# One pool of three PSUM couples for scores and maxima, two banks for weighted values, in a fused feed-forward / attention / feed-forward block

## The reference

```
x = x + 0.5 * ffn(layernorm(x))
x = x + attention(layernorm(x))
x = x + 0.5 * ffn(layernorm(x))       # the same ffn weights again

ffn(y):  g = y @ Wg.T ; u = y @ Wu.T            # Wg, Wu: 2048 x 256, 4-bit codes times a scale per 32
         return (gelu_tanh(g) * u) @ Wd.T        # Wd: 256 x 2048, the same coding
attention(y): q, k, v = y @ w_project.T          # 16 heads of 16
         a = softmax(causal(q k.T / 4)) ; return (a v) @ w_out.T
```

## Time and profile before

| | us |
|---|---|
| median of 3 runs (936.38 to 936.63) | 936.6 |
| the profiled execution | 936.64 |
| its span in the trace | 934.8 |
| PE, DVE, ACT busy | 903.2, 620.3, 471.1 |

### The profile page before, as it was taken

One profiled execution on the slowest core, in us unless ns is written; L12 is line 12 of the kernel. 1 busy time (PEld: TensorE's weight loads), 2 busy tenths in 40 slices (PEclk: granted clock), 3 DMA queues, 4 the chain that ended last, 5 costly groups with the idle time before them and its releaser, 6 DMA issues.

```text
span 934.8 us, 16016 instructions
## 1 busy us (share of the span) xinstructions
PE 903.2 (97%) x6214; PEld 395.3 (42%) x6214; DVE 620.3 (66%) x1008; ACT 471.1 (50%) x640; POOL 295.8 (32%) x510
## 2 busy tenths in 40 slices
PE   5999999999999999999999999999999999999998
PEld 3556445554534454223445322244532221445444
DVE  7994435758788688887687777778776650352221
ACT  2662342133264341786332699933269999441340
POOL 4767362233154240134241022224201110442240
PEclk9999999999999999999999999999999999999999
DMA  8000060050000060000050000000000000000000
GB/s 278 1 1 1 0 113 2 1 105 10 2 2 1 1 113 2 1 2 2 1 113 1 24 1 2 2 1 1 1 23 2 2 1 1 1 1 1 23 1 23
DMA packets 19770, 20.23 MB, mean 22 GB/s; under 512 B 3056, under 2 KB 18416, under 8 KB 19696
## 3 DMA queue, kind: packets, MB, share of 16 engines
q1 hardware_dynamic: 18048, 17.76, 8.4%
q10 hardware_dynamic: 1648, 1.44, 0.5%
HBM read 12.78 MB, written 6.29 MB: 20 GB/s over the span
## 4 chain that ended last, share of the span: by engine, by line
PE 84%; ACT 5%; DVE 5%; issue 4%; POOL 1%; DMA 0%; ACTq 0%; POOLq 0%; DVEq 0%
PE ps L997 13%; PE ps L999 12%; PE ps L998 12%; PE ps L1026 12%; PE ps L1192 10%; PE ps L1145 7%; PE ps L1027 6%; PE ps L1173 5%; ACT inter L629 5%; PE ps L984 1%; DVE sg L932 1%; DVE sg L935 1%; PE ps L1116 1%; PE ps L1108 1%; PE ps L1100 1%
## 5 line engine op out<-in xcount | busy, mean ns | idle before, releaser
L629 ACT ACTIVATE inter<-ps 128x1024 f32<-128x1024 f32 (+3 forms) x320 | 264.6, 897 | 105.0 <-PE ps L1173 103.0
L935 DVE TENSOR_REDUCE sg<-ps 128x2 f32<-128x1024 f32 (+3 forms) x223 | 224.6, 1039 | 46.5 <-PE ps L1145 23.6
L637 ACT ACTIVATE wreg<-ps,gelu_in 128x512 f32<-128x512 f32 x112 | 77.0, 687 | 255.2 <-PE ps L999 255.2
L519 POOL TENSOR_TENSOR inter<-wreg,inter 128x512 f16<-128x512 f32 x112 | 129.3, 1157 | 230.3 <-ACT inter L608 230.2
L1026 PE MATMUL ps<-wd,inter 128*128 128x512 f16 x512 | 169.8, 380 | 0.0
L511 POOL TENSOR_SCALAR_AFFINE_SELECT inter<-inter 128x128 f32<-128x128 f32 x256 | 67.0, 293 | 310.4 <-ACT inter L629 310.3
L804 DVE SCALAR_TENSOR_TENSOR wreg<-ps,kappa,wreg 128x512 f32<-128x512 f32 x128 | 95.4, 746 | 85.2 <-PE ps L999 81.6
L1192 PE MATMUL ps<-inter,v 128*17 128x512 f32 (+3 forms) x1280 | 146.0, 534 | 0.3 <-DVE oT L558 0.2
L1027 PE MATMUL ps<-wd,inter 128*128 128x256 f16 x512 | 139.6, 273 | 0.0
L932 DVE TENSOR_REDUCE sg<-ps 128x1 f32<-128x512 f32 (+3 forms) x194 | 113.1, 628 | 36.1 <-PE ps L1145 24.2
L1173 PE MATMUL ps<-qreg,kreg 50*128 50x512 f16 (+3 forms) x640 | 108.7, 351 | 8.3 <-ACT inter L629 4.8
(11 more groups left out here) (131 smaller groups left out, 847.1 us busy)
## 6 DMA issues: line engine op xcount, KB each, us to landing
qk_split<-oT SPq DMA_DIRECT2D x4, 1024.0 KB, 4.4
kreg<-qk_split SPq DMA_DIRECT2D x24, 128.0 KB, 4.2
qreg<-qk_split SPq DMA_DIRECT2D x24, 128.0 KB, 6.7
out_x<-xres SPq DMA_DIRECT2D x4, 512.0 KB, 3.0
xres<-in_L_attn_x SPq DMA_DIRECT2D x3, 512.0 KB, 8.8
kreg<-in_L_ffn_gate_W_packed SPq DMA_DIRECT2D x4, 256.0 KB, 5.4
kreg<-in_L_ffn_up_W_packed ACTq DMA_DIRECT2D x4, 256.0 KB, 7.1
kreg<-in_L_ffn_down_W_packed SPq DMA_DIRECT2D x1, 1024.0 KB, 9.7
```

The source lines that it names most:

```text
L519: pool.tensor_tensor(inter[:, 1, u, :], prod_ring[:, u % 3, :], inter[:, 0, u, :], ALU.subtract).then_inc(s_inter, 1)
L629: act.activation(p_slot(pair)[:, :, 0:w // EDGE, :], ps[:, 512 * b:512 * b + 1024].rearrange("p (a k q) -> p a k q", a=2, q=EDGE)[:, :, 0: ...
L935: dve.tensor_reduce(m_part[:, r, part, col:col + 9:8], both[:, :, 0:width], AX.X, ALU.max).then_inc(s_slot_read, 1)
```

## The change

Scores and maxima units of an attention stretch now take from one pool of three couples, (0,1), (2,3) and (6,7). Which couple each takes is written out in a second table, BANKS, beside a new PLAN; the rule of the table is that a claim takes the couple that was read first. Banks 4 and 5 are left to weighted values (one claim at a group's first step, kept to its last) and rows. DVE always reads a maxima unit with one instruction. On PE all the waits for a bank are worked out in one place (`freed`, `banks_read`): for each claim, which counter its last reader moves.

```diff
+        def two(at):
+            return ps[:, :].rearrange("p (b n) -> p b n", b=8)[:, at[0]:at[1] + 1:at[1] - at[0], :]
...
-        pair_bank = []
-        for b in range(2 * len(steps)):
-            k = b - max(f for f in first_pairs if f <= b)
-            pair_bank.append(0 if k < EARLY else 2 * ((k - EARLY + 1) % 2))
...
         PLAN = (
...
-            "pssmpssmmsppsmspsmsmssmspmspsmpsmssmspsspsmsppsmspsmspsmp",
+            "sspsmmmspssppsmmspsmspssmsmmmspsspsspssmpmsmpspsmspsmmpsspmm",
...
+        BANKS = (
+            "",
+            "",
+            "0167401236701230167230523014670123672301670123016723670123501672301236701236701423016723012367",
...
+            claims = {"scores": 2, "max": 2, "rows": 1, "pv": 1}
...
-                    elif kind in SLOTTED:
-                        at = tuple(5 + (ring + a) % 3 for a in range(2 if kind == "max" else 1))
-                        ring += len(at)
+                    elif kind in claims:
+                        at = tuple(next(banks) for _ in range(claims[kind]))
+                    if kind == "pv":
+                        sums = at
...
+        freed, reader = [], {b: ("residual", 1 + b + 1) for b in range(TPC)}
+        probs = reads = 0
+        for kind, n, u, at in order:
...
+            freed.append({name: max([reader[b][1] for b in mine if b in reader and reader[b][0] == name], default=0)
+                          for name in ("probs", "slot_read", "o_read", "residual")})
...
-                    if in_two(kind, at):
-                        for a in range(2):
-                            dve.tensor_reduce(m_part[:, r, part, col + 8 * a:col + 8 * a + 1], bank(at[a], width),
-                                              AX.X, ALU.max).then_inc(s_slot_read, 1)
-                    else:
-                        dve.tensor_reduce(m_part[:, r, part, col:col + 9:8], both[:, :, 0:width],
-                                          AX.X, ALU.max).then_inc(s_slot_read, 1)
+                    dve.tensor_reduce(m_part[:, r, part, col:col + 9:8], both[:, :, 0:width],
+                                      AX.X, ALU.max).then_inc(s_slot_read, 1)
...
+            def banks_read(free):
+                for name, signal in (("probs", s_p), ("slot_read", s_slot_read), ("o_read", s_o), ("residual", s_resid)):
+                    if free[name] > past[name]:
+                        pe.wait_ge(signal, free[name])
+                        past[name] = free[name]
...
-                if same_bank[b] >= 0:
-                    pe.wait_ge(s_p, same_bank[b] + 1)
-                pe.wait_ge(s_resid, 1 + (had["downs"] if pair_bank[b] else (had["downs"] - 1) // TPC * TPC + 2))
-                dst = [bank(pair_bank[b] + a, CT - q0) for a in range(2)]
+                banks_read(free)
+                dst = [bank(at[a], CT - q0) for a in range(2)]
```

More of the change, by code:

```diff
@@ L254, in the_order @@
             order = []
-            scores, values, maxima, chain = [], [], [], []
+            scores, values, maxima, chain, sums = [], [], [], [], None
             for t in range(len(steps)):
@@ L269, in the_order @@
                       "v": iter([("v", c, None) for c in range(NCH)])}
-            for (stretch, k), plan in zip(MAIN, PLAN):
-                turn, ring = 0, 0
+            claims = {"scores": 2, "max": 2, "rows": 1, "pv": 1}
+            for (stretch, k), plan, banks in zip(MAIN, PLAN, BANKS):
+                turn, banks = 0, iter(int(b) for b in banks)
                 if stretch == "ffn":
@@ L290, in macaron_block @@
         written = {(kind, n): k + 1 for k, (kind, n, _, _) in enumerate(slots) if kind != "max"}
-        def in_two(kind, at):
-            return kind == "max" and at not in ((4, 5), (6, 7))
-        freed_at, place, reads, latest = [], {}, 0, {}
-        for kind, n, u, at in slots:
-            freed_at.append(max(latest.get(b, 0) for b in at))
-            for k, b in enumerate(at):
-                latest[b] = reads + (k + 1 if in_two(kind, at) else 1)
-            reads += 2 if in_two(kind, at) else 1
-            if kind != "max":
-                place[kind, n] = reads
-        before, seen = [], {"pairs": 0, "groups": 0, "downs": TPC, "slots": 0, "low": 0, "projected": 0}
+        place = written
+        freed, reader = [], {b: ("residual", 1 + b + 1) for b in range(TPC)}
+        probs = reads = 0
+        for kind, n, u, at in order:
+            mine = at or ()
+            if kind in ("gate", "up"):
+                mine = (u + 2 * (kind == "up"),) if u < 2 else ()
+            elif kind == "pv" and steps[n][3]:
+                mine = ()
+            freed.append({name: max([reader[b][1] for b in mine if b in reader and reader[b][0] == name], default=0)
+                          for name in ("probs", "slot_read", "o_read", "residual")})
+            probs, reads = probs + (kind == "scores"), reads + (kind in SLOTTED)
+            if kind == "scores":
+                reader.update({b: ("probs", probs) for b in at})
+            elif kind in SLOTTED:
+                reader.update({b: ("slot_read", reads) for b in at})
+            elif kind == "pv":
+                reader[at[0]] = ("o_read", steps[n][0] + 1)
+            elif kind == "down" and u[1] == 3:
+                reader[u[0]] = ("residual", 1 + TPC * n + u[0] + 1)
+        before, seen = [], {"pairs": 0, "groups": 0, "downs": TPC, "slots": 0, "projected": 0}
         for kind, n, u, at in order:
@@ L315, in macaron_block @@
                 seen["slots"] += 1
-                if 4 in at:
-                    seen["low"] = sum(2 if in_two(x[0], x[3]) else 1 for x in slots[:seen["slots"]])
                 if kind == "project":
@@ L1084, in _, with planned @@
             pe.wait_ge(s_wl, len(groups))
-            slot = [0]
-            def planned(kind, n, unit, at, had):
+            past = {"probs": 0, "slot_read": 0, "o_read": 0, "residual": 0}
+            def banks_read(free):
[3 more added lines that the diff above has]
+                        past[name] = free[name]
+            def planned(kind, n, unit, at, free):
                 c, g = n // NG, n % NG
-                if freed_at[slot[0]]:
-                    pe.wait_ge(s_slot_read, freed_at[slot[0]])
-                if had["groups"] and at[0] == 4:
-                    pe.wait_ge(s_o, had["groups"])
+                banks_read(free)
                 if kind == "o":
@@ L1209, in _ @@
                 elif kind == "scores":
-                    scores(n, u, had)
+                    scores(n, u, at, free)
                 elif kind == "pv":
-                    weighted_values(n, had)
+                    weighted_values(n, at, free)
                 elif kind in SLOTTED:
-                    planned(kind, n, u, at, had)
+                    planned(kind, n, u, at, free)
 _INS = ["L0_attn_x", "L0_attn_w_project", "L0_attn_w_out", "L0_ffn_gate_W_packed", "L0_ffn_gate_scales",
```

103 lines of the change are left out of this document (59 added, 44 removed).

## The result

| | before | after |
|---|---|---|
| median | 936.69 (936.38 to 938.05, 14 runs) | 939.26 (937.53 to 941.01, 14 runs) |
| the profiled execution, its span | 936.64, 934.8 | 939.75, 938.0 |

The ratio is 1.002 with a 95% interval of 1.0013 to 1.0027: **slower by 0.2%**; the medians lie 2.6 us apart. I had forecast 935.5, that is 1.1 faster, with the highest of my three chances (0.41) on faster. The time lies in my range of 928.5 to 944.5, but on the other side of the kernel before.

A forecast was written before the change was run, and what follows sets the result against it. PE's steps set what attention stretches need, with 30.5 us more spent waiting for banks, and ACT needed in attention 3. Terms 0.5 - 0.9 - 1.1 - 1.5 + 0 + 1.9 = -1.1 gave 935.5 from 936.6; range 928.5 to 944.5.

The forecast's parts named there:

- the 162.5 that I wrote down as a sign: Attention 0 to 2 together: length expected to go from 161.8 to within 2 us of 162.5.
- Steps on PE: All ffn and attention stretches: same work, some units moved by the new lists; +0.5 us, sure to some 0.3.
- One scores unit earlier: Ffn 5 tail takes one scores unit from attention 3, relieving ACT; -0.9 us, or 0 if PE bounds there.
- A third couple for scores: Last quarter of attention 3, no maxima left: scores get three couples, not two; -1.1 us, bounds 0 and -4.3.
- One DVE read: Attention 0 to 2: 97 maxima units read once, not twice, saving DVE time; -1.5 us, bounds +3 and -6.
- The second bank for weighted values: Weighted values: removes the wait for their copy, for which PE waited 0.2 us in all; 0.
- The pool: Attention 0 to 2: fuller shared couples give a tenth more waiting; +1.9 us, bounds -10 and +10.
- The slow one: Attention: tight pool, PE's order couples ACT to DVE; 13 more early claims, +6.5 us, about 943; chance 0.32.
- the 15 I had named: Scores' weight loads: over 15 us of idle time released by DVE's reduce would speak for the tight pool.
- point of decision: Attention 2: the tight pool decides once PE's waits there pass some 10 us, from 7.4.
- Pooling pays: Attention: dedicated couples wasted room; a fifth of 30.5 us waiting goes, -6.1, about 930.5; chance 0.33.
- The rival in which the moved unit and third couple do nothing: Attention 3: PE bounds there too, so +2.0 on the sum, 937.5; no chance of its own given.

The follow-up runs named there:

- e6: Kernel before with only one scores unit moved from the head of attention 3 into the tail of ffn 5; 936.93 us, ratio 0.9987 to 1.0004.
- e17: Changed kernel with attention 3 alone put back to its old order, two scores couples and ring; 937.67 us, ratio 1.0003 to 1.0021.
- e20: The changed kernel run again without any edit, for comparison on the same chip; 938.99 us, ratio 1.001 to 1.0028.
- e5: Changed kernel with two DVE reads per maxima unit in attention stretches, couple freed after the second; 943.0 us, ratio 1.0047 to 1.0073.
- e3: Kernel before, ring and order unchanged, with every maxima unit read by one DVE instruction; 958.0 us, ratio 1.0204 to 1.0236.
- e9: Changed kernel with weighted values always on bank 4 and rows on bank 5; 942.35 us, ratio 1.0041 to 1.0066.
- e16: Changed kernel with old order and unshared couples: scores (0,1), (2,3), maxima (6,7), weighted values 4 and 5; 956.9 us, ratio 1.0185 to 1.0224.
- e1: Changed kernel with the PLAN of before and a BANKS table made for it by the same rule; 949.0 us, ratio 1.011 to 1.0146.
- e18: Changed kernel with the regular pattern of two scores, one weighted values in attention 3's tail; 938.20 us, ratio 1.0008 to 1.0025.
- e7: Changed kernel up to ffn 4, order, banks and reads of the kernel before from attention 2 on; 936.17 us, ratio 0.9986 to 1.0004.
- e21: Repeat of e7: changed kernel up to ffn 4, kernel before from attention 2 on; 937.18 us, ratio 0.9991 to 1.0009.

## Why the prediction was wrong, point by point

I forecast -1.1; in executions without a costly fall of the clock it is +1.3, and in the median +2.6.

*The sum itself.* The changes of PE's steps that I listed by stretch add up to +0.9, not the +0.5 that went into the sum. With +0.9 the sum is -0.7. Likewise my terms for attention 0 to 2 give 163.5 from 161.8, and not the 162.5 that I wrote down as a sign.

*Steps on PE.* Near in the ffn stretches: +0.4, -0.3, -0.2, -0.7 and +0.4 forecast for ffn 1 to 5, +0.5, -0.7, 0, -0.5 and +0.5 measured.

*One scores unit earlier (-0.9).* **This step failed.** e6 gives 0: attention 3 -0.3, ffn 5 +0.5. I let ACT bound the tail and forgot that the first stretch of attention 3 is not bounded by ACT but by PE, as the earlier trace rows shows with ACT idle 0.92 and 0.71 us. I had written the condition under which the gain is 0, and chosen the other.

*A third couple for scores (-1.1).* **This step failed too.** With the unit moved, attention 3 is 111.1 on the old order and two couples (e17) and 111.2 on the new order and three (e20), so the third couple with its order gains nothing. ACT's row of eight at 0.92 us had said that the tail was closed, and I took a quarter of all of ACT's idle time all the same, which lies elsewhere. These two steps, 2.0 us together, are the whole distance between -0.7 and +1.3; the ffn stretches and attention 0 to 2 were +1.3 together by my terms and came to +1.3.

*One DVE read (-1.5).* The sign was right inside the pool: two reads that free the couple together cost 3.7 more (e5, for 152 units), 1.4 of it in attention 2. But the other side of the edit, the first bank's early release, I priced within +3, and where its loss stands alone it costs 21 (e3). It didn't show in the sum because the pool and its order come with it.

*The second bank for weighted values (0).* Mis-sized: inside the changed kernel it is worth 3.1 us, 0.6, 1.6 and 1.0 of them in attention 0, 1 and 3 (e9). With the order of before it was not tried alone. I read the price from PE's wait of 0.2 for the copy. That was the wait of the old order, which leaves room at a group's end; the new one doesn't.

*The pool (+1.9).* For attention 0 to 2 my terms made +1.7 with the steps on PE (+1.3) and the reads, and +1.4 was measured, 163.2 against "within 2 us of 162.5". That agreement is luck. The place was not as I had it: -0.2, -0.2 and +1.8. And the parts behind it are six to fourteen times as large: over attention 0 to 2 one read alone adds 20 us (falls of the clock among them), sharing takes 10 off again and the new order 9 (the table of four steps above). In attention 2, the one stretch where 1.8 us are lost, maxima's waits rise by 3.8 and scores' fall by 2.0.

*The rivals.* The slow one had the right mechanism and direction: PE's order ties scores to DVE and maxima to ACT, and the 15.0 us of scores' weight loads behind DVE is right at the 15 I had named. Its point of decision, some 10 us of waits in attention 2, was not reached (9.9 by the claims, from 8.1), and its price was five times too high: 13 more early claims at 0.5 us, where the measured rise is 1.3 us. Pooling pays is false against the kernel before, but true against the same banks unshared (7.9 by the medians, e16 to e1). The rival in which the moved unit and third couple do nothing (937.5) is what the undisturbed executions are: 937.5 to 938.0.

*What nothing in my text provided for* is the granted clock. The changed kernel has steps of about 1.3 us in 17 of 25 runs, and the median sits one step up. That a fall makes a step is shown by the eight profiled executions above their lowest group that the section on the result lists: seven lie one step up with one costly fall, and one lies two up with two. Four of the eight have their only costly fall at 23.0 to 23.7 us, where the change has not begun. Whether the order of the change makes falls more frequent by its pauses in the tail stays open: e17 and e18 change that tail and still have 3 and 5 of 11 runs a step up, against 7 of 11 in e20, and the kernel before has from 1 in 15 to 12 in 27, by the set of runs.

## What to carry to other kernels

Two buffers' reach is set by how finely they are given back: three banks freed one by one are a buffer and a half, three banks freed as couples are one. An order written out by hand and the scheme of its buffers are one design, and a wait of 0.2 us in the old pair says nothing about the new one. A sum that comes out right over three stretches shows nothing about its terms while each of them is many times as large as what is left. Before a unit is credited as moved off a bounding engine, ask which engine bounds where it stood, and not which bounds the stretch.

## What the runs showed of the hardware

The granted clock fell to 0.50 for 3.4 us at places that differ between executions of one program: at 787.0 in one profile of the changed kernel and at 19.5 in the other. What a fall costs depends on the place: nothing at 19.5 (e20), 1.1 to 1.4 us at 23.0 to 23.7, 1.2 at 787.0, 1.5 at 416.6 and 416.8. Ahead of the fall at 787.0 PE was busy 2.69 of 4.00 us; e20 has 2.68 of 4.00 at the same place and kept its clock. In e18 it fell at 416.8 after a window in which PE was busy 4.09 of 4.80:

```profile
412.00:416.80 4.80, 4.09 (x42) 1.31 (x44) 4.33 (x4) 3.44 (x7) 3.18 (x12) 1.00 0.01 2
416.80:420.20 3.40, 3.40 (x31) 0.79 (x28) 1.78 (x4) 2.40 (x3) 0.00 (x0) 0.51 0.03 5
```

That one made attention 1 1.5 us longer (57.7 against 56.1). The busy share alone doesn't tell from these rows where the clock will fall. With steps of 1.3 us in a kernel of 937, a difference of 0.1% between two medians can be a matter of how often they come (e7 and e21 are one kernel, 936.17 and 937.18); the lowest groups of the same two, 935.9 to 936.2 and 936.1 to 936.2, agree.
